# Block attention on 32-row and 32-column tiles of TensorE, and two projection banks in the first head attention

## The reference

```python
q = (emb @ Wq.T).reshape(B, SQ, N_HEADS, KQ_DIM).transpose(0, 2, 1, 3)
k = (context @ Wk.T).reshape(B, SK, N_HEADS, KQ_DIM).transpose(0, 2, 1, 3)
v = (context @ Wv.T).reshape(B, SK, N_HEADS, KQ_DIM).transpose(0, 2, 1, 3)
q = _layernorm(q, qn_w, qn_b)
k = _layernorm(k, kn_w, kn_b)
attn = jax.nn.softmax(jnp.einsum('bhqd,bhkd->bhqk', q, k) * scale, axis=-1)
out = jnp.einsum('bhqk,bhkd->bhqd', attn, v)
return out.transpose(0, 2, 1, 3).reshape(B, SQ, N_HEADS * KQ_DIM) @ Wu.T + bu
```

```python
q, k, v = split_heads(x @ Wq), split_heads(x @ Wk), split_heads(x @ Wv)
scores = jnp.einsum('bhqd,bhkd->bhqk', q, k) / jnp.sqrt(jnp.float32(HD))
attn_w = jax.nn.softmax(scores, axis=-1)
ctx = jnp.einsum('bhqk,bhkd->bhqd', attn_w, v)
attn_out = ctx.transpose(0, 2, 1, 3).reshape(b, s, d) @ Wo + bo
out1 = _layernorm(x + attn_out, ln1_g, ln1_b)
```

## Time and profile before

| | us |
|---|---|
| median of 3 runs (1622.50 to 1624.17) | 1622.64 |
| the profiled execution | 1623.44 |
| its span in the trace | 1621.7 |
| PE busy in the span | 1397.8 |
| DVE busy | 839.1 |
| ACT busy | 728.3 |
| POOL busy | 146.7 |

### The profile page before, as it was taken

The page is one execution under the profiler, slowest core; times in us unless marked ns, Lnnn a source line. Parts: engine busy times, 40 slices in busy tenths (PEclk is TensorE's granted clock), DMA queues, the critical chain, the costliest instruction groups (busy, mean ns, idle before and its releaser), DMA issues. The chain is left out here.

```text
span 1621.7 us, 27487 instructions
## 1 busy us (share of the span) xinstructions
PE 1397.8 (86%) x9061; PEld 1085.9 (67%) x9061; DVE 839.1 (52%) x2258; ACT 728.3 (45%) x1657; POOL 146.7 (9%) x256
## 2 busy tenths in 40 slices
PE   6765689999998789959999997995499996999995
PEld 5631367777777457749999995994377773667664
DVE  4548466666664445445454553345777772122224
ACT  4341466666664311225555553342255551433433
POOL 1010000000000000000000002004233430000000
PEclk9878699999999799969999997996599995999998
DMA  8000000000000000000000001202000000000000
GB/s 323 1 1 0 1 1 2 1 1 1 1 1 1 1 1 1 1 0 1 1 2 1 1 1 43 75 2 104 0 1 1 0 1 0 1 1 1 0 1 26
DMA packets 6429, 24.55 MB, mean 15 GB/s; under 512 B 797, under 2 KB 1311, under 8 KB 5418
## 3 DMA queue, kind: packets, MB, share of 16 engines
q1 hardware_dynamic: 6314, 23.03, 4.1%
HBM read 21.98 MB, written 1.05 MB: 14 GB/s over the span
## 5 line engine op out<-in xcount | busy, mean ns | idle before, releaser
L1304 DVE SCALAR_TENSOR_TENSOR XN<-bank,gate,XN 128x128 f32<-128x128 f32 x256 | 89.9, 351 | 224.7 <-PE bank L1268 222.2
L1284 ACT ACTIVATE e_hidden<-bank,small 128x512 f32<-128x512 f32 x152 | 104.4, 687 | 214.5 <-PE bank L1256 214.5
L765 PE MATMUL bank<-a_va,a_pT 128*128 128x65 f32 x1024 | 130.3, 270 | 0.7 <-ACT a_pT L931 0.6
L1009 DVE TENSOR_REDUCE a_mx<-bank 128x4 f32<-128x512 f32 x128 | 87.8, 686 | 80.2 <-PE bank L805 80.1
L1268 PEld LDWEIGHTS bank<-attention_weights,e_hidden 128*128 128x128 f32 x1024 | 119.2, 192 | 14.8 <-issue 14.8
L765 PEld LDWEIGHTS bank<-a_va,a_pT 128*128 128x128 f32 x1024 | 125.2, 193 | 2.4 <-ACT a_pT L931 1.1
L1256 PE MATMUL bank<-XNT,attention_weights 128*128 128x512 f32 x256 | 121.2, 606 | 1.3 <-PEq L541 1.3
L1268 PE MATMUL bank<-attention_weights,e_hidden 128*128 128x128 f32 x1024 | 119.3, 275 | 0.0
L830 PE MATMUL bank<-attention_weights,a_cv 128*128 128x256 f32 x256 | 84.4, 411 | 15.5 <-issue 15.5
L931 ACT ACTIVATE a_pT<-bank 128x512 f32<-128x512 f32 x128 | 76.1, 595 | 41.9 <-PE bank L839 39.2
L1017 DVE TENSOR_TENSOR a_shifted<-bank,a_mx 128x512 f32<-128x512 f32 x128 | 88.3, 690 | 3.4
(11 more groups left out here) (351 smaller groups left out, 2718.2 us busy)
## 6 DMA issues: line engine op xcount, KB each, us to landing
attention_weights<-in_a SPq DMA_DIRECT2D x2, 2048.0 KB, 11.6
mod_ring<-in_mod_weights SPq DMA_DIRECT2D x4, 576.0 KB
ctx_both<-in_ctx SPq DMA_DIRECT2D x1, 2048.0 KB, 10.1
attention_weights<-in_up SPq DMA_DIRECT2D x1, 2048.0 KB, 7.6
attention_weights<-in_down SPq DMA_DIRECT2D x1, 2048.0 KB, 13.2
down<-in_down SPq DMA_DIRECT2D x1, 1536.0 KB, 18.5
down<-in_mod_weights SPq DMA_DIRECT2D x2, 576.0 KB
X<-in_x SPq DMA_DIRECT2D x4, 256.0 KB, 3.5
```

Source lines behind the costliest of these rows:

```text
L765: last = pe.matmul(value_bank[:, j * (W + 1):(j + 1) * (W + 1)], pT[:, i.slot(2), j * 128:(j + 1) * 128], va[:, p, g // 2 * 8 + 2 * j + g ...
L1009: dve.tensor_reduce(mx[:, i.slot(2), :], score_bank[i.slot(2)][:, :].rearrange("p (h s) -> p h s", h=4), AX.X, ALU.max).then_inc(maxed, 1)
L1284: act.activation(hidden[0:rows, p, f, :], up_bank_of(i, f)[0:rows, :], function, bias=up_bias(g, f)).then_inc(hidden_ready, 1)
L1304: dve.scalar_tensor_tensor(out=total, in0=down_bank[j][:, e * D:(e + 1) * D], scalar=gate_column(k, 4 * q + j, g * per_group + e), in1=tot ...
```

## The change

In the **first head attention** the projections get two banks (2 and 3) in turn, and the turned probabilities one (5) instead of two. The turning of `qn` and all that follows moves one phase later (lags 1, 2, 5, ... become 2, 3, 6, ...). The second head attention runs as before.

In the **block attention**
- POOL writes the masked keys once a batch (`own`: head j of each block of four) instead of four times, and the scores of group r are a matmul on the 32 rows of block r alone, 512 columns; two groups are issued together every other phase, into four score banks.
- The probabilities are turned by plain matmuls against the identity (two passes) instead of transpositions (one).
- The values of a whole batch are issued together: 16 matmuls with 32 columns of values stationary (8 features of one head among zeros) and the turned probabilities as 128 moving columns, each on one of four column tiles of 32, and 16 more with ones stationary for the sums. The result is already turned, so L1889 and L1961 go. DVE inverts 128 columns instead of 16.
- DVE's affine steps and the copy of the output move to POOL, which also clears two buffers (1,280 and 160 columns) at the start of the stage.
- `y` and the turned output share bank 7 with the projections, so their matmuls wait for `qkv_kept` of a later batch.

```diff
-        lag = {"square": 1, "turn_qk": 1, "keep_qk": 2, "scores": 5, "project_v": 5, "subtract": 5, "exponentials": 6,
-               "turn_p": 7, "keep_p": 7, "values": 9, "turn_o": 11, "out": 11, "normalise": 12, "turn_x": 12}
+        lag = {"square": 1, "turn_qk": 2, "keep_qk": 3, "scores": 6, "project_v": 6, "subtract": 6, "exponentials": 7,
+               "turn_p": 8, "keep_p": 8, "values": 10, "turn_o": 12, "out": 12, "normalise": 13, "turn_x": 13}
...
-        score_bank, turn_bank = [k.ps[0], k.ps[1]], [k.ps[2], k.ps[3]]
-        value_bank, project_bank, qkt_bank, out_bank = k.ps[4], k.ps[5], k.ps[6], k.ps[7]
+        score_bank, value_bank, qkt_bank, out_bank = [k.ps[0], k.ps[1]], k.ps[4], k.ps[6], k.ps[7]
+        project_bank, turn_bank = ([k.ps[2], k.ps[3]], [k.ps[5]]) if qk_norm is not None else ([k.ps[5]], [k.ps[2], k.ps[3]])
+        projects, turns = len(project_bank), len(turn_bank)
...
-                if i.older_than(1):
-                    await_count(pe, qk_normed if qk_norm is not None else qk_kept, m)
+                if i.older_than(projects):
+                    await_count(pe, qk_normed if qk_norm is not None else qk_kept, m + 1 - projects)
+                bank = project_bank[i.slot(projects)]
...
-    PROJECT, KEEP_QKV, BLOCKS, SCORE, EXP, TURN_P, VALUES, NORM_O, TURN_O, OUT, ADD, NORMALISE, KEEP, TURN_OUT = \
-        0, 1, 4, 3, 5, 5, 6, 6, 7, 7, 7, 8, 9, 10
+    PROJECT, KEEP_QKV, BLOCKS, SCORE, EXP, TURN_P, VALUES, NORM_O, OUT, ADD, NORMALISE, KEEP, TURN_OUT = \
+        0, 1, 2, 3, 5, 5, 6, 6, 7, 7, 8, 10, 10
+    AFFINE = 9
...
-        score_bank, turn_bank, value_bank = k.ps[0:2], k.ps[2:4], k.ps[4:6]
-        project_bank, side_bank = k.ps[6], k.ps[7]
+        chain, scaled_ready, copied = sem("chain"), sem("scaled_ready"), sem("copied")
+        out_ready, out_turned, out_kept = sem("out_ready"), sem("out_turned"), sem("out_kept")
+        score_bank, turn_bank, value_bank, project_bank = k.ps[0:4], k.ps[4:6], k.ps[6], k.ps[7]
+        turned_out = y_bank = project_bank[:, 384:512]
...
-            pool.memset(va[:, :, :, W:W + 1], 1.0).then_inc(cleared, 1)
+            pool.memset(va[:, :, :], 0.0).then_inc(cleared, 1)
+            pool.memset(ones[:, :], 0.0).then_inc(cleared, 1)
+            pool.wait_ge(cleared, 2)
+            pool.memset(ones[:, :].rearrange("p (j w) -> p j w", w=40)[:, :, 0:W], 1.0).then_inc(cleared, 1)
...
+                if i.alive and i.offset % 4 == 0:
+                    b = batch_of(i)
+                    n, p = b.number, b.slot(2)
+                    await_count(pool, qkv_kept, n + 1)
+                    if b.older_than(2):
+                        await_count(pool, scored, 4 * n - 4)
+                    elif n == 0:
+                        pool.wait_ge(own_ready, 1)
+                    pool.tensor_tensor(kD[:, p, :, :], kT[:, p, :].unsqueeze(1).to_broadcast([128, 4, S]),
+                                       own[:, :].unsqueeze(2).to_broadcast([128, 4, S]), ALU.mult).then_inc(k_spread, 1)
+                i = at(AFFINE)
+                if i.alive and i.offset % 4 == 3:
+                    b = batch_of(i)
+                    n, p = b.number, b.slot(2)
+                    await_count(pool, scaled_ready, n + 1)
+                    if b.older_than(2):
+                        await_count(pool, out_turned, n - 1)
+                        await_count(pool, copied, n - 1)
+                    pool.tensor_tensor(out[:, p, :], scaled[:, p, :], k.affine3(2), ALU.mult).then_inc(chain, 1)
+                    await_count(pool, chain, n + 1)
+                    pool.tensor_tensor(out[:, p, :], out[:, p, :], k.affine3(3), ALU.add).then_inc(out_ready, 1)
+                    await_count(pool, out_ready, n + 1)
+                    pool.tensor_copy(col(k.out1, n), out[:, p, :]).then_inc(copied, 1)
...
+                if i.alive and i.offset % 2 == 0:
...
-                    await_count(pe, k_spread, m + 1)
-                    if i.older_than(2):
-                        await_count(pe, subtracted, m - 1)
-                    pe.matmul(score_bank[i.slot(2)][:, :], qT[:, p, :],
-                              kD[:, p, 4 * g:4 * g + 4, :].rearrange("p h s -> p (h s)"), start=True,
-                              stop=True).then_inc(scored, 1)
-+                    await_count(pe, k_spread, b + 1)
+                    if i.older_than(4):
+                        await_count(pe, subtracted, m - 2)
+                    for r in (g, g + 1):
+                        rows = slice(32 * r, 32 * r + 32)
+                        pe.matmul(score_bank[r][:, :], qT[rows, p, :],
+                                  kD[rows, p, :, :].rearrange("p h s -> p (h s)"), start=True,
+                                  stop=True).then_inc(scored, 1)
...
+                    await_count(pe, p_kept, 4 * n + 4)
                     if b.older_than(1):
+                        await_count(pe, o_normed, n)
+                    else:
+                        pe.wait_ge(cleared, 3)
+                    for at_column, stationary, per_group in ((0, va[:, p, :], 160), (S, ones[:, :], 0)):
+                        for j in range(4):
+                            for c in range(4):
+                                first = c * per_group + 32 * j
+                                last = pe.matmul(value_bank[32 * c:32 * c + 32, at_column:at_column + S],
+                                                 stationary[:, first:first + 32], pT[:, p, c, j * 128:(j + 1) * 128],
+                                                 start=j == 0, stop=j == 3, tile_position=(0, 32 * c))
+                                if at_column and j == 3:
+                                    last.then_inc(weighted, 1)
...
-                        last = pe.transpose(turn_bank[p][:, j * 128:(j + 1) * 128],
-                                            probs[:, p, j * 128:(j + 1) * 128], k.ident)
+                        last = pe.matmul(turn_bank[p][:, j * 128:(j + 1) * 128],
+                                         probs[:, p, j * 128:(j + 1) * 128], k.ident, start=True, stop=True)
...
+                    await_count(pe, o_normed, b.number + 1)
+                    if b.older_than(1):
+                        await_count(pe, out_kept, b.number)
+                    await_count(pe, qkv_kept, min(b.number + 3, B) if isinstance(b.number, int) else b.number + 3)
+                    pe.matmul(y_bank, k.ones[0:1, :], k.bias3[0:1, :], start=True, stop=False)
+                    pe.matmul(y_bank, oT[:, :], k.w3[:, 384:512], start=False,
...
+                    if i.older_than(8):
+                        await_count(act, weighted, 4 * b - 4)
+                    act.activation(pT[:, q, g, :], turn_bank[p][:, :], ACT.Copy).then_inc(p_kept, 1)
...
-                    dve.reciprocal(rec[:, :], o[:, :, W:W + 1].rearrange("p h w -> p (h w)")).then_inc(inverted, 1)
+                    dve.reciprocal(rec[:, :], value_bank[:, S:2 * S]).then_inc(inverted, 1)
...
+                    dve.tensor_tensor(oT[:, :], value_bank[:, 0:S], rec[:, :], ALU.mult).then_inc(o_normed, 1)
```

More of the change, by code:

```diff
@@ L850, in project_qk @@
                 if qk_norm is not None:
-                    last = pe.matmul(project_bank[:, :], source[:, p, :],
+                    last = pe.matmul(bank[:, :], source[:, p, :],
                                      weight[:, half * 512:(half + 1) * 512], start=True, stop=True)
@@ L855, in project_qk @@
                         at_pair = (half * 4 + j) * 128
-                        last = pe.matmul(project_bank[:, j * 128:(j + 1) * 128],
+                        last = pe.matmul(bank[:, j * 128:(j + 1) * 128],
                                          weight[:, at_pair:at_pair + 128], source[:, p, :],
@@ L908, in keep_qk @@
                 await_count(act, qk_turned if qk_norm is not None else qk_projected, m + 1)
-                bank = qkt_bank if qk_norm is not None else project_bank
+                bank = qkt_bank if qk_norm is not None else project_bank[i.slot(projects)]
                 if g == 0 and i.older_than(8):
@@ L1914, in body @@
                     b = batch_of(i)
-                    await_count(pe, o_kept, b.number + 1)
-                    pe.matmul(side_bank[:, 128:256], k.ones[0:1, :], k.bias3[0:1, :], start=True, stop=False)
-                    pe.matmul(side_bank[:, 128:256], oT[:, :], k.w3[:, 384:512], start=False,
-                              stop=True).then_inc(y_done, 1)
+                    await_count(pe, o_normed, b.number + 1)
[4 more added lines that the diff above has]
+                    pe.matmul(y_bank, oT[:, :], k.w3[:, 384:512], start=False,
+                              stop=True).then_inc(y_done, 1)
+                i = at(TURN_OUT)
+                if i.alive and i.offset % 4 == 3:
+                    b = batch_of(i)
+                    await_count(pe, out_ready, b.number + 1)
```

(2 more changed lines are left out.)

113 lines of the change are left out of this document (36 added, 77 removed).

## The result

The changed kernel takes 1630.74 us (median of 5 runs, 1629.08 to 1632.27) against 1622.64 us: ratio 1.0053, interval 1.0039 to 1.0068. It is slower by 8 us, where 1626 was forecast; the time is in the range and on the likelier side. The profiled execution took 1629.08 us, the shortest of the five, with a span of 1627.3. Two terms of the sum were wrong by 10 and 13 us and nearly cancel, so that the forecast came so near is luck.

What follows compares the result with a forecast made beforehand. TensorE sets the pace in both stages; after the change a round with ACT sets part of the block attention. First attention -23.6, round +25, rest +2.3 gave +3.7 on 1623.44, so 1627.1, median 1626 us; range 1600 to 1658.

Steps and rivals of the forecast that it cites:

- First attention, a batch: First attention: waits before the projection go and weights load ahead, 1.26 us a batch, -17.6 over 14 full batches.
- Rival 4: First attention gains nothing, because the hole before L830 takes over what the other gives: +18, 1644 us; chance 0.08.
- First attention, the start: Start of the first attention: with two projections in flight DVE's idle time goes, -6 us including one added latency.
- Five such phases of 5.0 become six of 2.6: Start of the first attention: projections 5.01 us apart come 2.6 apart, the sixth being the extra lag; gives the -6.
- Pieces of TensorE's work: Block attention: scores pair 0.86 us, turning 0.90, values and sums 1.79, each tile-shape switch 0.2; work alone 9.6 a batch.
- Rivals 1 and 2: Block attention: 1, tile-shape changes cost nothing, 1612 us, chance 0.24; 2, column tiles by two, 1655, or serial, 1712, 0.13.
- The round: Block attention: exponentials, turning, keeping in sequence take 2.6 us; a batch goes from 10.7 to 12.3, +25 over 16.
- What hides the rest: Block attention: DVE's longer inversion and POOL's work are covered; clearing adds 1.3 us and the stage's end +1.
- rival 3: Block attention: the clock falls and half clock makes a batch over 17 us, +80 or more, 1700 us; chance 0.05.
- The row of 193 to 207: Profile window cited for rival 3: TensorE busy 8.57 of 14 us at full clock, then 0.57 in the next 4 us.

Runs made afterwards that it cites:

- second bank alone: Kernel before with only the changed kernel's first attention (second projection bank, extra phase of lag), block attention as before: 1589.17 us, ratio 0.979.
- shortened: Changed kernel with the probabilities turned by four transpositions in place of four plain matmuls: 1610.67 us, ratio 0.9929.
- opened: Changed kernel with ScalarE keeping turned probabilities after the next exponentials, VectorE's inversion behind its subtraction, projections behind the turning: 1583.72 us, ratio 0.9753.
- filling the holes: Changed kernel with four identity matmuls added in each of the two phases per batch where TensorE waits for exponentials: 1613.06 us, ratio 0.9937.

## Why the prediction was right, and where it was not

- *First attention, a batch*: -1.26 forecast, -1.24 measured; the L831 hole as said. Rival 4 is out.
- *First attention, the start*: -6 forecast. The second bank alone gives -33.4, so the start is -16. **The term was mis-sized**, in the step "Five such phases of 5.0 become six of 2.6". The first five phases are 1.8 to 2.8 long (2.14 in the mean), and it was not five that were long: until the twelfth a phase took 4.9 on average, since the one-bank chain set them all, and from the sixth to the twelfth it takes 3.9 now. The prediction took the later ones for full phases of TensorE. Half clock was 3.7 to 6 us of it.
- *Pieces of TensorE's work*: values 1.79 and a switch of 0.2 forecast, 1.89 measured with it; scores pair 0.86 + 0.2; turning 0.90 and 1.0 with its switch. Rivals 1 and 2 are out: a switch costs 0.1 to 0.2, and column tiles run four at once. The Trainium skill (TensorE: Matmul & The Clock Gate, "Packing small matmuls") has 2.38 times for three column tiles; the values estimated from that figure would have taken 2.3. The trace has 1.89, which decides against carrying the figure over.
- *The round*: 12.3 a batch forecast, 12.38 measured, and confirmed where it was shortened (12.38 to 10.44 in an undisturbed batch) and opened (12.38 to 10.21). That would be +1.66 x 16 = +26.6; with the three written-out batches at +1.36 it is +25.7, forecast +25.
- *What hides the rest*: the inversion is 0.96 (0.26 to 2.1 allowed) and in the changed kernel only the output of one batch waits for what follows it, 1.5 us; clearing `va` is 1.17, and the first exponentials come 1.9 us later in the stage than before (1.3 forecast for the clearing). Once the round was opened the same inversion did hold the exponentials: its cover was the round.
- *The clock*: rival 3 had it fall for the whole stage or not at all, with 0.05, and **this step failed**. The row of 193 to 207 was read as a yes or no; what came was a stage mostly at 2.4 GHz with five stretches at 1.2, and a longer one at its start, and filling the holes gave back 12 us. Nothing in the sum carried a part of a fall. The prediction also called the idle share nearer to the stage before than to that stretch. By its own numbers it lies halfway: busy 9.6 of 12.3 us is 78%, the stretch has 61% and the stage before 96%.

The account: -33.4 for the first attention; in the block stage +25.7 round, +12 clock, and the remaining 2.5 for start and drain, together +40.2 by the traces. -33.4 + 40.2 is +6.8 for the +8.1 measured; the 1.3 between them is less than the spread of the five runs (3.2). The forecast had -23.6 + 27.3. It missed the first by 10 us and the second by 13, in opposite directions. The mechanism of the round was right, and the closeness of the total was not earned.

## What to carry to other kernels

Look for a circle of two engines (one waits for the other's result of the group just handed over) before counting an engine's work: it sets the phase whatever either is relieved of, and one operation moved behind the next group's first step opens it, often to show the next in-order queue. Size a change at a pipeline's start by the phases until it is full, not until the touched step is past. Where a tuned TensorE gets holes, even short ones (1.4 and 0.9 us here), ask what half clock costs in part, and try filling the holes: a useless matmul in an idle slot paid for itself in the middle of a stage, and brought next to nothing at its start.

## What the runs showed of the hardware

- fp32 matmuls on four 32-column tiles run four at once when the tiles alternate (64 passes of 128 columns in 1.89 us with the switch), and about two at once in the mean when four of one tile follow each other (4.23 us).
- TensorE fell to 1.2 GHz five times in the middle of a stage in which it was never idle for over 1.5 us (77.92 us busy of the 93 before the first fall). With the holes filled (91.02 of 93 busy) it did not fall there, nor in the two kernels with 87.58 of 93 and 87.63 of 89. With transpositions it fell most: 0.80 and 0.77 in the windows above, whose busy times (80.16 of 93, 77.57 of 88) are lengthened by the half clock.
- An inversion of 128 x 128 takes 0.96 us on VectorE, a multiplication of the same size 0.29.
